# Where a threshold search keeps its bits, and which engine applies eight layer norms of a two-layer decoder kernel

## What is computed

```python
x = x + L0_attn (layernorm(x))        # one head, causal, softmax over the whole score matrix
x = x + L0_xattn(layernorm(x), ctx)   # quantised weights, 77 context rows
x = x + L0_ffn  (layernorm(x))        # 8 experts, each takes its 128 best tokens
x = x + L1_attn (layernorm(x))        # 16 heads of 64, causal
x = x + L1_xattn(layernorm(x), ctx)   # 16 heads of 8, softmax over the 32 largest of 77 scores
x = x + L1_ffn  (layernorm(x))        # 8 experts, each token takes its 2 best

def _layernorm(x, axis=-1, eps=1e-05):
    m = jnp.mean(x, axis=axis, keepdims=True)
    v = jnp.var(x, axis=axis, keepdims=True)
    return (x - m) / jnp.sqrt(v + eps)

# the choice of tokens in L0_ffn
route_prob = jax.nn.softmax(xf @ Ws + bs, axis=-1).T
route_vals, routes = jax.lax.top_k(route_prob, k)       # k = 1024 / 8 = 128 per expert
```

## Time and profile before

| what | value |
|---|---|
| median of 3 runs | 599.43 us (599.36 to 604.56) |
| the profiled execution's own time | 599.37 us |
| its span, first to last instruction | 597.6 us |
| mean granted TensorE clock | 0.971 of full |
| busy: PE, DVE, ACT, POOL | 529.2, 394.8, 303.7, 223.4 us |

### The profile page before, as it was taken

One profiled execution on the slowest core, in us unless ns is written; L12 is line 12 of the kernel. 1 busy time (PEld: TensorE's weight loads), 2 busy tenths in 40 slices (PEclk: granted clock), 3 DMA queues, 4 the chain that ended last, 5 costly groups with the idle time before them and its releaser, 6 DMA issues.

```text
span 597.6 us, 12126 instructions
## 1 busy us (share of the span) xinstructions
PE 529.2 (89%) x3954; PEld 415.6 (70%) x3954; DVE 394.8 (66%) x2200; ACT 303.7 (51%) x760; POOL 223.4 (37%) x227
## 2 busy tenths in 40 slices
PE   4888859997899899988999898978898889999997
PEld 2565426874667656677677576767777778999997
DVE  3565685534342597966597999885968788744643
ACT  2341313434786676765775656745775554322222
POOL 5015850001433446653455545552732433340000
PEclk9996889999999999999999988989999999999999
DMA  4600012634000000000000000002520000010000
GB/s 119 201 1 15 27 40 73 181 102 158 2 1 1 1 2 1 1 3 2 2 1 2 2 1 2 2 2 68 181 66 10 15 15 19 19 32 2 27 1 10
DMA packets 24088, 21.03 MB, mean 35 GB/s; under 512 B 2175, under 2 KB 18643, under 8 KB 24027
## 3 DMA queue, kind: packets, MB, share of 16 engines
q1 hardware_dynamic: 23515, 19.21, 10.8%
q0 software_dynamic: 512, 1.05, 0.6%
HBM read 17.22 MB, written 3.03 MB: 34 GB/s over the span
## 4 chain that ended last, share of the span: by engine, by line
PE 62%; DVE 17%; ACT 11%; issue 6%; POOL 3%; DMA 1%; DVEq 0%; ACTq 0%; POOLq 0%
PE ps L1827 52%; PE ps L2220 4%; DVE wk L1185 3%; DVE nmax L1127 2%; ACT w_mem L1579 2%; DVE top L1175 2%; PE ps L2282 2%; ACT prT L1592 2%; DVE sel_mem L1009 2%; ACT f_mem L1544 1%; POOL xs_dram L785 1%; PE ps L2474 1%; PE ps L1839 1%; DVE xn L1148 1%; DVE xn L853 1%
## 5 line engine op out<-in xcount | busy, mean ns | idle before, releaser
L1127 DVE TENSOR_REDUCE nmax<-ps 128x2 f32<-128x256 f32 (+1 forms) x64 | 51.2, 821 | 60.7 <-PE ps L1827 59.0
L1185 DVE MATCH_REPLACE8 wk<-top,wk 128x77 f32<-128x77 f32 x384 | 80.6, 224 | 0.0
L702 POOL TENSOR_TENSOR w_mem<-w_mem,rinv 128x256 f32<-128x256 f32 (+3 forms) x44 | 53.3, 1222 | 51.6 <-DVE rinv L1133 51.0
L1306 DVE TENSOR_TENSOR sel_mem<-gr,ps 128x512 f32<-128x512 f32 x47 | 32.2, 686 | 47.1 <-ACT gr L1769 46.4
L1769 ACT ACTIVATE gr<-ps 128x512 f32<-128x512 f32 x47 | 28.1, 598 | 62.2 <-PE ps L1827 62.2
L1175 DVE MAX8 top<-wk 128x8 f32<-128x77 f32 x384 | 58.0, 224 | 0.1
L1827 PE MATMUL ps<-cat_mem 64*128 64x256 f32 (+7 forms) x276 | 55.7, 476 | 1.5 <-ACT cat_mem L1563 1.5
L731 POOL TENSOR_SCALAR wk<-wk 128x616 f32<-128x616 f32 x16 | 28.1, 1754 | 58.2 <-DVEq L1189 57.9
L1579 ACT ACTIVATE w_mem<-ps,nmax 128x128 f32<-128x128 f32 (+3 forms) x88 | 44.5, 520 | 10.3 <-DVE nmax L1127 10.2
L1827 PE MATMUL ps<-prT,cat_mem 128*64 128x128 f32 x640 | 43.5, 284 | 0.5 <-ACT xnT L1596 0.5
L626 POOL TENSOR_TENSOR rstd<-var_eps,minus_half 128x4 f32<-128x4 f32 x8 | 8.2, 1025 | 93.2 <-DVE var_eps L846 93.1
(11 more groups left out here) (350 smaller groups left out, 1345.1 us busy)
## 6 DMA issues: line engine op xcount, KB each, us to landing
w_mem<-in_L_ffn_W_dram SPq DMA_DIRECT2D x12, 256.0 KB, 3.2
f_mem<-in_L_ffn_Wg_dram SPq DMA_DIRECT2D x8, 256.0 KB, 2.7
f_mem<-in_L_ffn_Wu_dram SPq DMA_DIRECT2D x8, 256.0 KB, 3.1
f_mem<-in_L_ffn_Wd_dram SPq DMA_DIRECT2D x8, 256.0 KB, 3.9
sel_mem<-slot_dram SPq DMA_DIRECT2D x7, 256.0 KB
sel_mem<-in_L_ffn_W_dram SPq DMA_DIRECT2D x4, 256.0 KB, 4.1
xs_dram<-zero SPq DMA_DIRECT2D x1, 960.0 KB, 6.5
ys_dram<-f_mem SPq DMA_DIRECT2D x15, 64.0 KB, 1.5
```

The source lines that it names most:

```text
L702: pool.tensor_tensor(pr[s][:, :, at:at + n], pr[s][:, :, at:at + n], rinv[:, i % 8, :].unsqueeze(2).to_broadcast([P, 2, n]), ALU.mult)\
L1127: dve.tensor_reduce(nmax[:, i % 8, :], ps[:, 2 * s:2 * s + 2, at:at + (c + 1) * P], X, ALU.max, negate=True).then_inc(nmax_ready, 1)
L1185: dve.match_replace(wk[q][:, t, h, :], top[q][:, t, h, 8 * r:8 * r + 8], src[:, t, h, :], GONE).then_inc(top_step, 1)
L1306: dve.tensor_tensor(hg[s][:, :], gr[s][:, :], ps[:, 2 * s + 1, :], ALU.mult)\
```

## The change

Two things are changed.

In the search, `low` and `begun` become int32 views of three columns of PSUM bank 5; `digit`, `trial` and `digits` stay in SBUF. No instruction is added, removed or moved there.

In the eight norms Q0 to G3 the application goes from VectorE to ScalarE: xn = Identity(rstd * x + offset), with offset = -mean * rstd. VectorE computes `minus_mean` beside `var_eps`, waits until both are written, and then signals GpSimd with an instruction of its own (before, the signal rode on `var_eps`). GpSimd waits for its own power and multiplies to get `offset`. The norms of layer 0 and the first of layer 1 stay as they were.

```diff
--- before.py
+++ after.py
@@ -310,6 +310,8 @@
         mean_var = sb("mean_var", [P, NT, 2])
         var_eps = sb("var_eps", [P, NT])
         rstd = sb("rstd", [P, NT])
+        minus_mean = sb("minus_mean", [P, NT])
+        offset = sb("offset", [P, NT])
 
         VEC = {"a0_bq": 0, "a0_bk": 1, "x0_bq": 2, "x0_bk": 3, "x1_bq": 4, "x1_bk": 5, "b1": 6}
         NV = 6 + E * FC
@@ -429,9 +431,9 @@
         count = sb_early("count", [P, 8])
         flag16 = sb_early("flag16", [P, 1], bf16)
         digit = sb_early("digit", [P, 1], i32)
-        low = sb_early("low", [P, 2], i32)
+        low = ps[:, 5, 0:2].bitcast(i32)
         trial = sb_early("trial", [P, 1], i32)
-        begun = sb_early("begun", [P, 1], i32)
+        begun = ps[:, 5, 2:3].bitcast(i32)
         least = sb_early("least", [P, E])
         picks = sb_early("picks", [P, 2, NT + 1, E], bf16)
         ranks = sb_early("ranks", [P, 2, NT + 1, E])
@@ -707,7 +709,9 @@
 
                 pool.wait_ge(var, k + 1)
                 t = slice(2 * k, 2 * k + 2)
-                pool.tensor_tensor(rstd[:, t], var_eps[:, t], minus_half[:, t], ALU.pow).then_inc(ready, 1)
+                pool.tensor_tensor(rstd[:, t], var_eps[:, t], minus_half[:, t], ALU.pow).then_inc(pool_step, own.up())
+                pool.wait_ge(pool_step, own.now())
+                pool.tensor_tensor(offset[:, t], minus_mean[:, t], rstd[:, t], ALU.mult).then_inc(ready, 1)
 
             def add_bo(k):
 
@@ -1140,13 +1144,10 @@
                     dve.bn_aggr(mean_var[:, t, :], bn[:, t, :]).then_inc(dve_step, own.up())
                 dve.wait_ge(dve_step, own.now())
                 t = slice(2 * k, 2 * k + 2)
-                dve.tensor_scalar(var_eps[:, t], mean_var[:, t, 1], EPS, None, ALU.add).then_inc(var, 1)
-
-            def apply_two(k, rstd_done, ready):
-                dve.wait_ge(rstd_done, k + 1)
-                for t in (2 * k, 2 * k + 1):
-                    dve.tensor_scalar(xn[:, t, :], x[:, t, :], mean_var[:, t, 0:1], rstd[:, t:t + 1],
-                                      ALU.subtract, ALU.mult).then_inc(ready, 1)
+                dve.tensor_scalar(minus_mean[:, t], mean_var[:, t, 0], -1.0, None, ALU.mult).then_inc(dve_step, own.up())
+                dve.tensor_scalar(var_eps[:, t], mean_var[:, t, 1], EPS, None, ALU.add).then_inc(dve_step, own.up())
+                dve.wait_ge(dve_step, own.now())
+                dve.sem_inc(var, 1)
 
             def add_attention(k, source):
 
@@ -1221,9 +1222,6 @@
                     row_max(U + 2)
                 if U + 1 < NU:
                     row_inv(U + 1)
-                for k in range(3):
-                    if U == STAGE[k + 1] + 2:
-                        apply_two(k, qn_rstd, qn_ready)
                 for k in range(2):
                     if U == OUT[k]:
                         context_norm(k)
@@ -1244,8 +1242,6 @@
                 for k in range(2):
                     if U == OUT[k] + 1:
                         add_context(k, ps[:, 6, 0:2 * P])
-                    if U == OUT[k] + 2:
-                        apply_two(k, gn_rstd, gn_ready)
 
 
             def gates(i, first, n, bank):
@@ -1381,8 +1377,6 @@
                     add_attention(3, ps[:, 5, 0:2 * P])
                     places()
                     tiles_to_experts()
-                if b == 1:
-                    apply_two(3, qn_rstd, qn_ready)
                 if b == 2:
                     shares()
                 cross(b)
@@ -1392,8 +1386,6 @@
                     context_norm(2)
                 if j == 5:
                     add_context(2, ps[:, 4, 0:2 * P])
-                if j == 6:
-                    apply_two(2, gn_rstd, gn_ready)
                 if j == 10:
                     gates(1, 4, 2, 4)
                 if j == 12:
@@ -1409,8 +1401,6 @@
                     context_norm(3)
                 if i == 6:
                     add_context(3, ps[:, 4, 0:2 * P])
-                if i == 7:
-                    apply_two(3, gn_rstd, gn_ready)
                 if i == 11:
                     gates(2, 6, 2, 4)
                 if i == 13:
@@ -1599,6 +1589,12 @@
                 act.wait_ge(qc_ps, k + 1)
                 act.activation(qc[:, 2 * P * (k % 2):2 * P * (k % 2 + 1)], source, ACT.Identity, bias=bias("x1_bq"))\
                    .then_inc(qc_ready, 1)
+
+            def apply_two(k, rstd_done, ready):
+                act.wait_ge(rstd_done, k + 1)
+                for t in (2 * k, 2 * k + 1):
+                    act.activation(xn[:, t, :], x[:, t, :], ACT.Identity, bias=offset[:, t:t + 1], scale=rstd[:, t:t + 1])\
+                       .then_inc(ready, 1)
 
             def evac_cn(k, source):
                 act.wait_ge(cnT_ps, k + 1)
@@ -1676,6 +1672,12 @@
                 if U + 2 < NU:
                     exps(U + 2)
                 evac_pt(U)
+                for k in range(3):
+                    if U == STAGE[k + 1] + 2:
+                        apply_two(k, qn_rstd, qn_ready)
+                for k in range(2):
+                    if U == OUT[k] + 2:
+                        apply_two(k, gn_rstd, gn_ready)
                 if U == 4:
                     norm_T(7)
                 if U == 11:
@@ -1780,6 +1782,8 @@
                 for k in range(2):
                     evac_lo(b, k, F_BANKS[b % 2][k])
                 cross_two(b)
+                if b == 1:
+                    apply_two(3, qn_rstd, qn_ready)
                 if b == 2:
                     norm_two(3, qnT_ps, qnT_ready, four)
                 if b == 3:
@@ -1798,6 +1802,8 @@
                 cross_two(E + j)
                 if j == 3:
                     evac_cn(2, four)
+                if j == 6:
+                    apply_two(2, gn_rstd, gn_ready)
                 if j == 7:
                     norm_two(2, gnT_ps, gnT_ready, four)
                 if j == 9:
@@ -1813,6 +1819,8 @@
                 cross_two(E + NS + i)
                 if i == 4:
                     evac_cn(3, four)
+                if i == 7:
+                    apply_two(3, gn_rstd, gn_ready)
                 if i == 8:
                     norm_two(3, gnT_ps, gnT_ready, four)
                 if i == 9:
```

## The result

The changed kernel took 590.97 us (median of four executions: 589.41, 590.93, 591.01, 594.67) against 599.6 for the kernel before: ratio 0.9868, 95% interval 0.9819 to 0.9918. The forecast was 596.7 with a range down to 593.2, so it missed. The profiled execution took 589.41 us, span 587.6.

A forecast was written before the change was run, and what follows sets the result against it. TensorE was taken to hold 62% of the chain that ended last. Search -2.4, Q0 +0.7, G0 -1.25, G1 -0.05 and Q3 +0.3 summed to -2.7 us from 599.43, giving 596.7 us, range 593.2 to 599.4.

The forecast's parts named there:

- The bound: Whole kernel: TensorE holds 62% of the chain that ended last, VectorE 17%; VectorE changes pay only on that chain.
- term 1: Search: with low and begun in PSUM, ORs stop waiting for GpSimd, rounds 2.13 us instead of 2.46; -2.4 us.
- the search does not gain: Rival: in the search, PSUM costs what the freed port gave; 599.1 us, chance 0.10.
- Q0: Norm where TensorE waits for xn: ScalarE applies it behind evac_pt, so TensorE's transposes start later; +0.7 us.
- G0: Norm in unit 38: row maxima start earlier without xn on VectorE, but ScalarE's evacuations limit the gain; -1.25 us.
- VectorE's relief pays more: Rival: the norm in unit 38 gives its full 2.1 us and Q2 half that; 594.8 us, chance 0.08.
- G2: Late norm where ScalarE mostly waits for TensorE: nobody waits for what VectorE is freed of; 0 us.
- Q1, Q2, G3: Three norms where ScalarE waits for TensorE anyway, so its added xn work is covered; 0 us.
- ScalarE becomes the bound: Rival: in the attention loop ScalarE's xn delays TensorE; 598.0 us, or 599.3 with two more norms uncovered; chance 0.10.
- G1 and Q3: Two norms: -0.05 us at the first, held by evac_pt; +0.3 at the second, where token placing and GpSimd's scatter come later.
- The sum: Whole kernel: the search's gain and the norms' gains and costs together; -2.7 us.
- TensorE's clock does better: Rival: one or two stretches at 1.2 GHz fewer, 1.65 us each, in the changed part; 595.0 or 593.4 us, chance 0.17.

The follow-up runs named there:

- norms alone: The changed kernel with low and begun back in SBUF: 600.72 us, ratio 0.9983 to the kernel before; on repetition 600.99 us, ratio 0.9998.
- two tiles: The kernel before with two more unused 128x8 tiles in SBUF, no instruction changed: 599.87 us, ratio 0.996 to the kernel before.
- filled: The kernel before with six TensorE fillers, three of them new, placed earlier in layer 0's cross attention: 597.62 us, ratio 0.9956.
- search-only kernel: The kernel before with low and begun in PSUM, norms still on VectorE: 592.34 us, ratio 0.9848; on repetition 597.69 us, ratio 0.9856.
- experiment 5: The changed kernel with one TensorE filler in each search round instead of four: median 595.37 us against 595.86 for the changed kernel beside it.

## Why the prediction was wrong, by its steps

- **The bound and term 1** (the search): right in kind, and in size for the execution it was read from. -2.51 us (20.03 to 17.52) against -2.4; rounds of 2.13 as worked out; PSUM costs VectorE nothing (`trial` 0.15 us with a PSUM input, 0.16 without). As an estimate by the Trainium skill, "VectorE: DVE Perf Modes", section "The TRN2 errata — SBUF-src ops pay a fixed extra latency per instruction", a PSUM source would have cost 65 ns more; no row shows it, and the measurement decides. The rival "the search does not gain" is out. But the size holds for a search that begins at 67 us. Where it begins at 61 to 65, bits in SBUF took 21.9, 22.3 and 22.7 us (norms alone, two tiles, filled) and bits in PSUM 17.5 to 17.7: -4.4 to -5. Term 1 (-2.4) was mis-sized for those executions, since the row of GpSimd's L676 was not looked at as a thing that the search could meet.
- **Q0**: +0.9 for +0.7. ScalarE's pair took 0.87 where 0.65 was put (479 to 512 ns each, not the 369 of the earlier trace rows, which has one pointer operand where xn has two).
- **G0**: -1.5 for -1.25, and through the queue named: evac_v in front of the exponentials. TensorE's wait of 2.08 fell to 0.39. The rival "VectorE's relief pays more" is out at the two places that it names: at G0 VectorE had the 2.2 us and ScalarE let 1.3 through, and Q2 gives nothing. But relief of VectorE did pay more, at G2. The follower of `var_eps` was 0.31 later (344.93 - 344.55 - 0.07), for 0.35.
- **G2**: -1.1 for 0. This step failed by its mechanism. "What G2 frees on VectorE nobody waits for" was read from the share of waits in which ScalarE waits for TensorE; but VectorE stood idle 1.80 us in front of xn, fell behind by it, and TensorE's transposes of `sel_mem` then followed VectorE (timelines above).
- **Q1, Q2, G3**: 0. Q2 lets VectorE run 2.1 us ahead in one unit (offset -7.9 to -10.0) and is back at -7.9 two units on. "ScalarE becomes the bound" is out: where it takes the context out of PSUM it still waits for TensorE, as in the earlier trace rows, now (waits of the changed kernel, 187 to 396 us: total us, times, longest)

```profile
ACT sel_mem L1624 <- PE ps L1835: 8.2, 7, 1.8
```

  and behind 410 us, as in the earlier trace rows,

```profile
ACT gr L1771 <- PE ps L1835: 59.9, 41, 2.7
```

- **G1 and Q3**: in the first pair low stretches of the changed kernel lie on them (391 to 395 and 408 to 419 us). The changed kernel with Q0 on VectorE has none behind 392 us: there ScalarE's copies of G1 and Q3 (`xnT`) start 20.58 us apart, against 20.24 to 20.26 in five profiles with the norms on VectorE. That is Q3's +0.3 as forecast. G1's copy itself comes 0.2 us earlier than the search-only kernel's at its place, for the -0.05 forecast. Together +0.1.
- **The sum**, -2.7, lies within -3.0 ± 0.7 at equal low clock. By its steps it is short: the places give -2.5 + 0.9 - 1.5 - 1.1 + 0.1 = -4.1, most of the gap being G2. That the adjusted total comes so near the forecast is partly luck.
- **The step that failed** is the base under the sum, with the rival "TensorE's clock does better". The forecast took one execution's low clock for the kernel's and let it move only behind the search: one or two stretches fewer, 1.65 us each, with chance 0.17. It counted four stretches there; the trace of before has five (from 85, 310, 348, 369 and 396 us, the first twice as long), and two more ahead of the search (from 48 and 61 us, 13.6 us together) that it left out of account. Those two were missing in the first profile of the changed kernel, and 5.4 of its 10.0 us stand there. In low clock the two profiles are 34.7 and 18.8 us, at 0.40 a difference of 6.4 us. The changed kernel's mean over 20 executions, 594.3, lies within the range given; the first comparison's 591.0, of four executions, three of them among the six fastest of its 22, does not.
- **Open**: how the change comes to have less low clock. In the mean it is 7.0 ± 3.3 us less (5.6 ± 4.3 over all executions), more than chance would give, so part of it belongs to the change, and it is not the norms': norms alone has 4.4 ± 2.9 us more. With bits in SBUF and an early start the clock fell inside the search in all three profiles that had the full `xp` work (67 to 78 us); with `low` and `begun` in PSUM and four fillers a round, in none of ten before 78. But low clock inside the search costs next to nothing (experiment 5), so this does not say where the time comes from. The way from the search to the time by the clock is argued, not shown.

## What to carry to other kernels

Before summing terms, ask how much the kernel's time moves by itself: the mean granted clock of each timed execution is there to be read, and a difference of two profiles should be split at the first changed instruction. A wait of one instruction for another engine's instruction, without a semaphore, has no fixed price; look up every long instruction of that engine that can slide over it when the work before runs earlier or later. And a gain on one engine is worth what the next engine's queue lets through. Before putting such a gain at nothing, look two or three steps on: an engine that idles in front of the instruction to be moved may be late for something behind it.

## What the runs showed that was not expected

- A VectorE OR of one column with both inputs in SBUF waited across several GpSimd instructions in a row: it started at 65.37, behind which GpSimd ended an instruction at about 65.8, and ran until 67.80. The Trainium skill, "SBUF — State Buffer", section "SBUF: two separate sides", lets whichever of the two starts first have the pair of ports for its whole instruction and blocks the other; the 0.47 and 1.20 us of norms alone agree with that, each ending with a GpSimd subtraction, and the 2.43 us are longer than one instruction of 1.25.
- Half speed is nearly free where TensorE waits for VectorE: 16.6 us more low clock at the same median (experiment 5), against 0.40 us for each us over the executions of before.
- An ACTIVATE of 128x128 takes 0.27 us without a pointer operand, 0.37 with one (in the profile of before), and 0.49 with two, scale and bias (xn in the changed kernel). The first two read PSUM and xn reads SBUF, so the last step is not the pointer's alone for certain.
